# Attention probabilities and values in row tiles of 32 instead of 64, with the banks and one queue's loads rearranged

## The chip, the cores and the metric

The kernel runs on one core of one Trainium2 chip. The metric is the device time of one execution in microseconds; three executions of the kernel before took 294.55, 294.67 and 294.55 us, median 294.55 us. PE is TensorE (its weight loads are PEld), DVE is VectorE, ACT is ScalarE, POOL is GpSimd, SP is the engine whose queue issues every DMA of this kernel.

## The reference

Eight batches of 256 queries attend to 77 context rows each (16 heads of 64, model width 256), then pass a gated feed-forward layer of hidden width 768. Cut to what matters:

```
x = x + tanh(gate) * (softmax((LN(LN(x)) @ w_q) @ (ctx @ w_k).T / 8) @ (ctx @ w_v) @ w_out + b_out)
x = x + (silu(LN(x) @ wg.T) * (LN(x) @ wu.T)) @ wd.T
```

## The kernel before

Everything is float32; where a product is made of three rounded ones (hi times hi, lo times hi, hi times lo), the operands were split into `_hi` and `_lo` by ACT and by DVE or POOL. w_q and w_k are folded with the context into `t_all` ahead of the loop, so the scores of a batch are `xn` times `t`. V is computed once, stored to a scratch tensor in DRAM, and loaded again batch by batch.

A round of the loop treats one batch: its attention, the feed-forward layer of the batch before, and the first scores of the batch after. The order on each engine is written out by hand as a list of stage names (PE_ORDER, DVE_ORDER, ACT_ORDER, POOL_ORDER, SP_ORDER; the names ending in FIRST, START and END hold the order of the first and last rounds). Each engine works through its list strictly in that order, and waits on semaphores counted per batch.

A batch's attention has four units u: head group g = u // 2 (8 heads each) and query half t = u % 2. Per unit:
- S (`scores`, PE, lines 822 to 830): two halves of 4 heads x 77 keys, 6 matmuls each, into one bank of PSUM each. `score_bank` takes SCORE_BANKS in turn; a half waits until DVE has subtracted out of the bank's previous user.
- M (`maxima`, DVE, lines 1375 and 1380): the maxima of both halves, then both subtractions into `probs`. E (ACT, line 1075): the exponential. Z (`sums`, DVE, lines 1389 and 1392): sum and reciprocal.
- P (`normalise`, POOL, lines 1245 and 1253): multiplies by the reciprocals. Two neighbouring heads make a row of 154 keys, whose middle 128 are transposed as they lie (`probs`), and whose 13 at either end go to `rest`.
- T (`transpose_probs`, PE, lines 845 and 848): four transposes and one for the rest, C (ACT, lines 1086 and 1090) copies them to `pt`.

Per head group, V (`values`, PE, line 863) multiplies by the values: 16 float32 products of a 64-row (or 52-row) by 64-column tile of values with 256 queries, each of which the trace shows as two weight loads and two matmuls, 32 per call. They go to banks 4 and 5 (`ps_p`). O0 and O1 of ACT and DVE (lines 1102 and 1400) split the result into `o_hi` and `o_lo`; O0 and O1 of PE (`project`, lines 990 to 994) project it.

G0 to G5 (`gate_up`, line 921, 8 matmuls each), H (`hidden`, DVE, lines 1416 and 1419; the buffer of two makes H wait for POOL's h, line 1271, of two before), D (`down`, lines 974 and 977) and Y (DVE, line 1439) are the feed-forward layer. X1T and XT (lines 888 and 879) transpose the two normalised inputs, LN1 and LN of DVE (lines 1489 and 1432) make them, X1 of DVE (line 1406) splits the first of them. These users share three banks, MISC_BANKS, in the order of PE_ORDER; `last_user` says what each must wait for.

SP's queue, in SP_ORDER: RES loads the residual (line 557), V the values of the next batch (lines 586 and 595, once the present batch's V1 has read the old ones), LN the next input `x_ln` (line 562), OUT stores a result (line 571). In the start, `load_v(0)` is interleaved with the stores of V's five row blocks (line 648); ACT's copy of the last row block (line 1046) reuses the room of the third and waits until its store has landed.

Of the kernel before, what the change touches and what calls it, by code (L numbers as in the profile page):

```python
# [23 lines left out]
F32 = mybir.dt.float32  # L24
# [12 lines left out]
MISC_BANKS = (6, 7, 3)  # L37
SCORE_BANKS = (0, 1, 2)
LAST_BANKS = (4, 5, 7, 6, 0, 1)
LAST_X1T_BANKS = (0, 2)  # L40
LAST_DOWN_BANKS = (2, 3)
# [11 lines left out]
DVE_ORDER = "LN1 M2 LN Z2 X1 M3 O0 H0 Z3 H1 H2 M0 H3 H4 O1 Z0 H5 M1 R0 Z1 R1 AG Y0 Y1".split()  # L53
# [27 lines left out]
V_BANKS = (4, 5, None, 2, 3, 4, 5, 4, 3, None)  # L81
# [8 lines left out]
def xattn_ffn_kernel(nc, x, ctx_in, ln_gamma, ln_beta, w_q, w_kv, w_out, b_out, gate,  # L90
# [31 lines left out]
    NEXT = HALVES * K  # L122
    assert KEYS_WHOLE + NEW == K
    V_LOADS = HALVES + HG
    assert HALVES * KEYS_WHOLE == P and 0 < HR * NEW <= KEYS_WHOLE
# [8 lines left out]
    with whole:  # L134
# [52 lines left out]
        with before_loop:  # L187
# [6 lines left out]
            sb("gap", [P, 160 + 2 * IC * D], where=before_loop)  # L194
# [15 lines left out]
        v_rest = sb("v_rest", [P, 2, HR * DH])  # L210
# [5 lines left out]
        sb("pt_gap", [P, (HG - HR - 1) * Q - ROOMS * P])  # L216
# [16 lines left out]
        hid = sb("hid", [P, 2, Q])  # L233
        stats = sb("stats", [P, NT, 6])
# [61 lines left out]
        shared = [n for n in PE_ORDER if n in ("X1T", "XT", "G0", "G1", "G2", "G3", "G4", "G5", "D0", "D1", "O0", "O1")]  # L296
        bank = {n: MISC_BANKS[i % len(MISC_BANKS)] for i, n in enumerate(shared)}

        def last_user(b, name):

            at = shared.index(name) - len(MISC_BANKS)
            while at >= 0:
                n, k = shared[at], int(shared[at][1]) if shared[at][1].isdigit() else 0
                if n == "XT" and not (isinstance(b, int) and b >= B - 1):
                    return xn_done, DC * (b + 2)
                if n[0] == "O" and not (isinstance(b, int) and b == B):
                    return x1_done, NT * b + k + 1
# [104 lines left out]
        def gate_up_psum(b, f):  # L412

            return ps[:, LAST_BANKS[f], :] if last(b) else ps[:, bank[f"G{f}"], :]

# [123 lines left out]
        def _(sp):  # L539
# [33 lines left out]
            def load_v_whole(n):  # L573
# [9 lines left out]
                whole_keys = (slice(NEW, K), slice(0, KEYS_WHOLE))  # L583
                for r in range(HALVES):
                    half = slice(r * KEYS_WHOLE, (r + 1) * KEYS_WHOLE)
                    sp.dma_start(v_whole[half].rearrange("k g (j d) -> k (g j) d", d=DH),
                                 v_rows[whole_keys[r]].rearrange("k (h r d) -> k r h d", r=HALVES, d=DH)[:, r]).then_inc(v_in, 16)

            def load_v_rest(n, r, heads=range(HR)):
                v_rows = v_scratch.rearrange("(b k) n -> b k n", k=K)[n]  # L590
                by_head = v_rows.rearrange("k (g j r d) -> k r j g d", g=2, r=HALVES, d=DH)
                rest_keys = (slice(0, NEW), slice(KEYS_WHOLE, K))
                for j in heads:
                    first = r * KEYS_WHOLE + j * NEW
                    sp.dma_start(v_rest[first:first + NEW, :, j * DH:(j + 1) * DH], by_head[rest_keys[r], r, j]).then_inc(v_in, 16)

            def load_v(n):
                load_v_whole(n)
                for r in range(HALVES):
                    load_v_rest(n, r)  # L600
# [34 lines left out]
            out_rows = w_out.rearrange("(g n e r d) m -> e g r d n m", g=2, e=2, r=HALVES, d=DH)  # L635

            def load_wo(*which):
                for i in which:
                    for e in range(2):
                        sp.dma_start(wo_raw[e * DH:(e + 1) * DH, 2 * i:2 * i + 2, :],  # L640
                                     out_rows[e, i // HALVES, i % HALVES]).then_inc(s_in["wo"], 16)

            load_ln(1)
            load_wo(0, 1, 2)
            for r in range(RC):
# [4 lines left out]
                if r == 0:  # L650
                    load_wo(3)
                if r == 1:
                    sp.wait_ge(s_vrow[0], 16)
                    load_v_whole(0)
                    load_v_rest(0, 0, range(HR - 1))
                if r == 2:
                    load_v_rest(0, 0, range(HR - 1, HR))
                    load_v_rest(0, 1, range(HR // 2))
                if r == 3:
                    load_v_rest(0, 1, range(HR // 2, HR))  # L660
# [9 lines left out]
        def _(pe):  # L670
# [136 lines left out]
            def scores(b, u):  # L807
# [6 lines left out]
                if isinstance(b, int) and b == 0 and u == 1:  # L814
                    evacuated(pe, first_v + V_BANKS.index(SCORE_BANKS[2]))
# [17 lines left out]
            def transpose_probs(b, g, t):  # L833
# [10 lines left out]
                for j in range(HR):  # L844
                    ins = nc.tensor.transpose(ps_p[:, 0, j * P:(j + 1) * P], probs[:, u, j * NEXT + NEW:j * NEXT + NEW + P], ident[:])  # L845
# [4 lines left out]
            def values(b, g):  # L850
# [5 lines left out]
                for pair in range(2):  # L856
                    for keys in (v_whole, v_rest):
                        for e in range(2):
                            j = 2 * pair + e
                            at = j if keys is v_whole else HR  # L860
                            for r in range(HALVES):
                                half = slice(r * KEYS_WHOLE, r * KEYS_WHOLE + (KEYS_WHOLE if keys is v_whole else HR * NEW))
                                ins = mm(ps_p[e * DH:(e + 1) * DH, r, pair * Q:(pair + 1) * Q],  # L863
                                         keys[half, g, j * DH:(j + 1) * DH], pt[half, at, :],
# [714 lines left out]
```

## Time and profile before

| | |
|---|---|
| median of three executions | 294.55 us |
| the profiled execution | 294.75 us |
| its span, first to last instruction | 292.9 us |
| one steady round | 28.28 us |
| PE busy in the span | 97% |
| DVE, POOL, ACT busy | 79%, 59%, 54% |

What lies between 292.9 and 294.75 us is before the first and after the last instruction. Matmuls overlap each other by design (a matmul's start to the next one's is shorter than its duration), so starts are what to compare on PE. The granted TensorE clock is full in all 40 slices.

### The profile page before, as it was taken

The numbers are of one execution on the slowest core, as the hardware profiler recorded it, in microseconds if no ns is written. First come the engines' busy times: TensorE is split into PE (matmuls) and PEld (weight loads), VectorE is DVE, ScalarE is ACT, GpSimd is POOL, SyncE is SP. The second block draws the span as 40 slices with busy tenths as digits, with TensorE's granted clock in tenths as the row PEclk, the third lists the DMA queues.
The fourth block names the chain that finished last, engine by engine and source line by source line (L and its number), as shares of the span: only waits on it lengthen the run. The fifth ranks groups of instructions, "written<-read, shape, count | busy, mean of one in ns | idle before, by whom it ended". The sixth has DMA issues, their size and how long they took to land.

```text
span 292.9 us, 6761 instructions
## 1 busy us (share of the span) xinstructions
PE 283.7 (97%) x2513; PEld 261.9 (89%) x2513; DVE 230.9 (79%) x609; ACT 157.3 (54%) x311; POOL 173.3 (59%) x199
## 2 busy tenths in 40 slices
PE   8999999999789999999999999999999999999995
PEld 7999978878788899989898989898989899988994
DVE  1598897787778689878986898789778987885873
ACT  3657875567047733863385349435932683156052
POOL 2644875369668690968196639654964587237133
PEclk9999999999999999999999999999999999999999
DMA  6995138522414013001201120112011101110001
GB/s 201 374 369 169 36 106 256 175 71 110 147 43 145 3 42 110 1 23 37 97 0 39 43 74 0 40 41 74 1 41 49 66 3 40 42 36 2 0 32 46
DMA packets 26668, 23.32 MB, mean 80 GB/s; under 512 B 12602, under 2 KB 24866, under 8 KB 26634
## 3 DMA queue, kind: packets, MB, share of 16 engines
q1 hardware_dynamic: 26634, 22.86, 25.1%
q8 instruction: 22, 0.36, 0.5%
q14 instruction: 12, 0.10, 0.1%
HBM read 15.87 MB, written 4.62 MB: 70 GB/s over the span
## 4 chain that ended last, share of the span: by engine, by line
PE 90%; DVE 5%; ACT 1%; issue 1%; POOL 0%; DVEq 0%
PE ps L921 12%; PE ps L863 10%; PE ps L822 6%; PE ps L830 6%; PE ps L826 6%; PE ps L990 5%; PE ps L994 5%; PE ps L991 5%; PE ps L746 5%; PE ps L845 4%; PE ps L974 3%; PE ps L977 3%; PE ps L942 2%; PE ps L754 2%; PE ps L756 2%; PE ps L755 2%
## 5 line engine op out<-in xcount | busy, mean ns | idle before, releaser
L1245 POOL TENSOR_TENSOR probs<-probs,total 128x512 f32<-128x512 f32 x32 | 33.6, 1050 | 60.6 <-DVE total L1392 60.5
L1260 POOL TENSOR_TENSOR t_lo<-t_all,t_hi 128x1232 fp32r<-128x1232 f32 x16 | 45.7, 2857 | 3.0 <-ACT t_hi L1114 3.0
L1271 POOL TENSOR_TENSOR h_lo<-hid,h_hi 128x256 fp32r<-128x256 f32 x42 | 30.7, 738 | 21.1 <-ACT h_hi L1158 21.1
L1086 ACT COPY pt<-ps 128x512 f32<-128x512 f32 x32 | 19.1, 597 | 40.3 <-PE ps L845 40.3
L990 PE MATMUL ps<-wo_hi,o_hi 128*128 128x256 f32 x128 | 36.4, 284 | 0.0
L991 PE MATMUL ps<-wo_lo,o_hi 128*128 128x256 f32 x128 | 36.1, 282 | 0.0
L994 PE MATMUL ps<-wo_hi,o_lo 128*128 128x256 f32 x128 | 35.9, 281 | 0.0
L1102 ACT CAST o_hi<-ps 128x512 fp32r<-128x512 f32 x32 | 17.2, 590 | 25.1 <-PE ps L863 25.1
L822 PE MATMUL ps<-t_hi,xn_hi 128*128 128x308 f32 x128 | 30.7, 321 | 0.0
L1389 DVE TENSOR_REDUCE total<-probs 128x8 f32<-128x616 f32 x32 | 25.3, 791 | 6.3 <-ACT probs L1075 5.5
L1375 DVE TENSOR_REDUCE top<-ps 128x4 f32<-128x308 f32 x64 | 28.3, 471 | 2.3 <-PE ps L830 2.3
L1075 ACT ACTIVATE probs<-probs 128x616 f32<-128x616 f32 x32 | 23.2, 726 | 12.2 <-DVE probs L1380 12.2
L1400 DVE TENSOR_TENSOR o_lo<-ps,o_hi 128x512 fp32r<-128x512 f32 x32 | 20.6, 685 | 10.7 <-ACT o_hi L1102 10.2
L830 PE MATMUL ps<-t_hi,xn_lo 128*128 128x308 f32 x128 | 28.5, 304 | 0.0
L826 PE MATMUL ps<-t_lo,xn_hi 128*128 128x308 f32 x128 | 28.4, 303 | 0.0
L1380 DVE TENSOR_TENSOR probs<-ps,top 128x308 f32<-128x308 f32 x64 | 27.3, 467 | 0.0
L1158 ACT CAST h_hi<-hid 128x256 fp32r<-128x256 f32 x42 | 17.9, 426 | 14.5 <-DVE hid L1419 14.5
L990 PEld LDWEIGHTS ps<-wo_hi,o_hi 128*128 128x128 f32 x128 | 24.0, 187 | 0.4 <-issue 0.4
L994 PEld LDWEIGHTS ps<-wo_hi,o_lo 128*128 128x128 f32 x128 | 24.3, 190 | 0.0
L991 PEld LDWEIGHTS ps<-wo_lo,o_hi 128*128 128x128 f32 x128 | 24.1, 188 | 0.0
L1416 DVE SCALAR_TENSOR_TENSOR hid<-tanh_g,ps 128x256 f32<-128x256 f32 x42 | 17.0, 404 | 8.2 <-POOL h_lo L1271 4.6
L822 PEld LDWEIGHTS ps<-t_hi,xn_hi 128*128 128x128 f32 x128 | 20.2, 189 | 2.9 <-issue 2.7
(171 smaller groups left out, 836.3 us busy)
## 6 DMA issues: line engine op xcount, KB each, us to landing
x_ln<-in_x SPq DMA_DIRECT2D x8, 256.0 KB, 2.9
v_scratch<-v_out SPq DMA_DIRECT2D x4, 512.0 KB, 3.4
v_whole<-v_scratch SPq DMA_DIRECT2D x16, 128.0 KB
stream<-in_x SPq DMA_DIRECT2D x8, 256.0 KB, 3.5
x_rooms<-in_x SPq DMA_DIRECT2D x7, 256.0 KB, 7.8
out<-stream SPq DMA_DIRECT2D x7, 256.0 KB, 2.2
wk_raw<-in_L_xattn_w_kv SPq DMA_DIRECT2D x4, 256.0 KB, 5.2
wq_raw<-in_L_xattn_w_q SPq DMA_DIRECT2D x1, 1024.0 KB, 7.6
```

The lines of the kernel that those rows point to most:

```text
L822: mm(o, xn_hi[:, c, qs], t_hi[:, c, cols], start=c == 0, stop=False)
L826: mm(o, xn_hi[:, c, qs], t_lo[:, c, cols], start=False, stop=False)
L830: ins = mm(o, xn_lo[:, c, qs], t_hi[:, c, cols], start=False, stop=c == DC - 1)
L863: ins = mm(ps_p[e * DH:(e + 1) * DH, r, pair * Q:(pair + 1) * Q], keys[half, g, j * DH:(j + 1) * DH], pt[half, at, :], start=keys is v_who ...
L921: ins = mm(o[:, at:at + Q], whole(w[:, c, fs], general), whole(x2[:, c, :], general), start=x2 is x2_hi and c == 0, stop=x2 is x2_lo and c ...
L990: mm(o, o_hi[:, i, ts], wo_hi[:, i, :], start=i == 0, stop=False)
L991: mm(o, o_hi[:, i, ts], wo_lo[:, i, :], start=False, stop=False)
L994: ins = mm(o, o_lo[:, i, ts], wo_hi[:, i, :], start=False, stop=i == IC - 1)
L1245: nc.gpsimd.tensor_tensor(whole, whole, scale.to_broadcast([P, HR, HALVES, KEYS_WHOLE]), ALU.mult).then_inc(probs_done, 1)
L1260: nc.gpsimd.tensor_tensor(t_lo[:, :, cols], t_all[:, :, n, cols], t_hi[:, :, cols].bitcast(F32), ALU.subtract).then_inc(tlo_done, 1)
L1271: nc.gpsimd.tensor_tensor(h_lo[:, f, :], hid_of(b, f), h_hi[:, f, :].bitcast(F32), ALU.subtract).then_inc(hlo_done, 1)
L1375: nc.vector.reduce_max(top[:, u, heads[r]], psum[r], AXIS_X).then_inc(max_done, 1)
```

## The change

The keys of a batch are no longer split as 64 and 13 in pairs of heads, but as 64 = 2 x 32 (`a`) and 13. The four row quarters `c` of a tile hold four heads: `packed` (two new buffers, by turns) holds 8 heads x 32 keys of half 0 in its first 256 columns and of half 1 in the last 256; a transposed 128-column block is then four heads' 32 keys. `rest` puts two heads' 13 keys into each quarter. V makes 24 products of 32 rows x 64 columns instead of 16 of 64 or 52: each quarter c writes its own bank (the V entry of MISC_BANKS, and 3, 4, 5), its two heads e the upper and lower 64 partitions. The scores have two banks instead of three. V0 and V1 join the users of MISC_BANKS. H3 is moved ahead of M0 on DVE. SP loads `v_whole` in 8 DMAs of 32 rows instead of 2 of 64; `v_rest` stays at 8.

```
-MISC_BANKS = (6, 7, 3)
-SCORE_BANKS = (0, 1, 2)
+MISC_BANKS = (6, 7, 2)
+SCORE_BANKS = (0, 1)
+VALUE_BANKS = (3, 4, 5)
...
-DVE_ORDER = "LN1 M2 LN Z2 X1 M3 O0 H0 Z3 H1 H2 M0 H3 H4 O1 Z0 H5 M1 R0 Z1 R1 AG Y0 Y1".split()
+DVE_ORDER = "LN1 M2 LN Z2 X1 M3 O0 H0 Z3 H1 H2 H3 M0 H4 O1 Z0 H5 M1 R0 Z1 R1 AG Y0 Y1".split()
...
-V_BANKS = (4, 5, None, 2, 3, 4, 5, 4, 3, None)
+V_BANKS = (4, 5, None, 3, 7, 4, 5, 4, 3, None)
...
-        shared = [n for n in PE_ORDER if n in ("X1T", "XT", "G0", ...)]
+        shared = [n for n in PE_ORDER if n in ("X1T", "XT", "V0", "V1", "G0", ...)]
...
+                if n[0] == "V":
+                    return olo_done, NU * b + 2 * k + 1
...
-                for r in range(HALVES):
-                    half = slice(r * KEYS_WHOLE, (r + 1) * KEYS_WHOLE)
-                    sp.dma_start(v_whole[half]..., v_rows[whole_keys[r]]...).then_inc(v_in, 16)
+                for a in range(PARTS):
+                    for c in range(HR):
+                        sp.dma_start(v_whole[quarter(c), a].rearrange("k (f d) -> k f d", d=DH), by_bank[a, c]).then_inc(v_in, 16)
...
-                    ins = nc.tensor.transpose(ps_p[:, 0, j * P:(j + 1) * P], probs[:, u, j * NEXT + NEW:j * NEXT + NEW + P], ident[:])
+                    ins = nc.tensor.transpose(ps_p[:, 0, j * P:(j + 1) * P], packed[(NU * b + u) % ROOMS][:, j * P:(j + 1) * P], ident[:])
...
-                for pair in range(2):
-                    for keys in (v_whole, v_rest):
-                        for e in range(2):
-                            for r in range(HALVES):
-                                ins = mm(ps_p[e * DH:(e + 1) * DH, r, pair * Q:(pair + 1) * Q],
-                                         keys[half, g, j * DH:(j + 1) * DH], pt[half, at, :],
-                                         start=keys is v_whole, stop=keys is v_rest)
+                claim(b, f"V{g}")
+                for a in range(PARTS):
+                    for c in range(HR):
+                        for e in range(HALVES):
+                            mm(ps[e * DH:(e + 1) * DH, value_bank(g, c), 0:Q],
+                               v_whole[quarter(c), a, (HALVES * g + e) * DH:(HALVES * g + e + 1) * DH],
+                               pt[quarter(c), HALVES * a + e, :], start=a == 0, stop=False)
+                for c in range(HR):
+                    for e in range(HALVES):
+                        ins = mm(ps[e * DH:(e + 1) * DH, value_bank(g, c), 0:Q],
+                                 v_rest[quarter(c), g, e * DH:(e + 1) * DH], pt[quarter(c), HR, :], start=False, stop=True)
...
-                    nc.scalar.copy(o_hi[:, 2 * n:2 * n + 2, :],
-                                   ps_p[:, i, :].rearrange("p (i q) -> p i q", i=2)).then_inc(ohi_done, 1)
+                    nc.scalar.copy(o_hi[:, value_chunks(g, i), :], value_psum(g, i)).then_inc(ohi_done, 1)
...
-                nc.gpsimd.tensor_tensor(whole, whole, scale.to_broadcast([P, HR, HALVES, KEYS_WHOLE]),
-                                        ALU.mult).then_inc(probs_done, 1)
+                wait(pool, pt_done, n + 1 - ROOMS)
+                nc.gpsimd.tensor_tensor(packed[n % ROOMS][:].rearrange("p (a h k) -> p h a k", a=PARTS, h=HG), whole,
+                                        scale.to_broadcast([P, HG, PARTS, ROWS]), ALU.mult).then_inc(probs_done, 1)
```

`value_chunks` and `value_psum` give the first copy of each group one bank (256 columns) and the second three (768), where both had 512; DVE's split follows them. `load_wo` brings w_out's rows in the new order of heads with 4 DMAs instead of 8. The rotation of MISC_BANKS becomes X1T 6, V0 7, XT 2, G0 6, G1 7, G2 2, G3 6, G4 7, G5 2, V1 6, O0 7, O1 2, D0 6, D1 7; it was X1T 6, XT 7, G0 3, G1 6, G2 7, G3 3, G4 6, G5 7, O0 3, O1 6, D0 7, D1 3.

## Rows read from the trace of the kernel before

**Rows 1.** The page: busy time of the engines, share of the span, instructions.
```profile
PE 283.7 (97%) x2513; PEld 261.9 (89%) x2513; DVE 230.9 (79%) x609; ACT 157.3 (54%) x311; POOL 173.3 (59%) x199
```
**Rows 2.** Busy time by stretch: one steady round (us, PE, PEld, DVE, ACT, POOL, granted clock, DMA).
```profile
139.60:167.90 28.30, 28.30 (x262) 26.44 (x262) 23.61 (x66) 15.42 (x32) 17.89 (x18) 1.00 0.14 39
```
**Rows 3.** Timeline of PE around one call of V (start us, us, engine, line, ...).
```profile
127.37 0.66 PE L863 MATMUL ps<-pt,v_whole 64*64 64x256 f32 x8
127.86 0.61 PE L863 MATMUL ps<-pt,v_rest 52*64 52x256 f32 x8
128.29 0.61 PE L863 MATMUL ps<-pt,v_whole 64*64 64x256 f32 x8
...
129.27 0.41 PE L822 MATMUL ps<-t_hi,xn_hi 128*128 128x308 f32 x1
```
**Rows 4.** The same call, first 0.05 us and first 0.2 us alone: weight loads, matmuls.
```profile
127.37 0.15 PEld L863 LDWEIGHTS ps<-pt,v_whole 64*64 64x64 f32 x4
127.37 0.45 PE L863 MATMUL ps<-pt,v_whole 64*64 64x256 f32 x4
```
**Rows 5.** Timeline of SP's queue after V1 of a steady round.
```profile
129.40 1.24 SPq L586 DMA_DIRECT2D v_whole<-v_scratch  x2
...
137.36 0.51 SPq L562 DMA_DIRECT2D x_ln<-in_x  x1
```
**Rows 6.** By line: SP's time to issue (min/median/max ns); 13, 64, 128 partitions.
```profile
L595 SPq DMA_DIRECT2D v_rest<-v_scratch x64: 782/782/935, 48.6 to 249.7; - x64
L586 SPq DMA_DIRECT2D v_whole<-v_scratch x16: 538/600/1314, 47.3 to 243.1; - x16
L562 SPq DMA_DIRECT2D x_ln<-in_x x7: 368/512/513, 38.6 to 222.2; - x7
```
**Rows 7.** The page: DMA issues, KB, us from issue to landing.
```profile
x_ln<-in_x SPq DMA_DIRECT2D x8, 256.0 KB, 2.9
```
**Rows 8.** Timeline of DVE in the first third of a steady round.
```profile
142.50 0.85 DVE L1380 TENSOR_TENSOR probs<-ps,top 128x308 f32<-128x308 f32 x2
143.27 0.73 DVE L1432 TENSOR_SCALAR x_hat<-x_ln,mean,rstd 128x256 f32<-128x256 f32 x2
144.14 0.80 DVE L1389 TENSOR_REDUCE total<-probs 128x8 f32<-128x616 f32 x1
145.09 0.64 DVE L1406 TENSOR_TENSOR x_lo<-ps,x_hi 128x512 fp32r<-128x512 f32 x1
146.41 0.85 DVE L1380 TENSOR_TENSOR probs<-ps,top 128x308 f32<-128x308 f32 x2
```
**Rows 9.** Lines by form (count, busy us, mean ns): one subtraction; a split of 256 columns.
```profile
L1380 DVE TENSOR_TENSOR probs<-ps,top 128x308 f32<-128x308 f32 x64 | 27.3, 467 | 0.0
L1524 DVE TENSOR_TENSOR x_lo<-ps,x_hi 128x256 fp32r<-128x256 f32 x2 | 0.8, 422 | 0.0
```
**Rows 10.** Timeline of PE in the same third: S3 and G0 begin.
```profile
142.80 0.53 PE L822 MATMUL ps<-t_hi,xn_hi 128*128 128x308 f32 x2
146.99 0.49 PE L921 MATMUL ps<-x_hi,wg 128*128 128x256 f32 x2
```
**Rows 11.** The chain that ended last: G0 to G2 of one round (start us, us).
```profile
118.95 2.86 PE ps L921 x24
```
**Rows 12.** Timelines of DVE (H3) and PE (V1) of a steady round.
```profile
155.13 0.42 DVE L1416 SCALAR_TENSOR_TENSOR hid<-tanh_g,ps 128x256 f32<-128x256 f32 x1 [0.57 <-POOL h_lo L1271]
155.59 0.42 DVE L1419 TENSOR_TENSOR hid<-hid,ps 128x256 f32<-128x256 f32 x1
...
155.65 0.66 PE L863 MATMUL ps<-pt,v_whole 64*64 64x256 f32 x8
```
**Rows 13.** Timelines of ACT and PE in the start.
```profile
54.41 0.59 ACT L1046 COPY v_out<-ps 104x512 f32<-104x512 f32 x1 [1.36 <-DMA v_scratch<-v_out]
...
56.83 0.59 ACT L1086 COPY pt<-ps 128x512 f32<-128x512 f32 x1
...
57.57 0.63 PE L845 MATMUL ps<-ident,probs 128*128 128x128 f32 x4
```

More of the change, by code:

```diff
@@ L193, in xattn_ffn_kernel @@
             kt_lo = sb("kt_lo", [P, IC, CR], F32R, where=before_loop)
-            sb("gap", [P, 160 + 2 * IC * D], where=before_loop)
+            sb("gap", [P, 2 * IC * D - 96], where=before_loop)
             wg_raw = sb("wg_raw", [P, FC, D], where=before_loop)
@@ L292, in xattn_ffn_kernel @@
         xres_biased, xnlo_done = sem("xres_biased"), sem("xnlo_done")
-        shared = [n for n in PE_ORDER if n in ("X1T", "XT", "G0", "G1", "G2", "G3", "G4", "G5", "D0", "D1", "O0", "O1")]
+        shared = [n for n in PE_ORDER if n in ("X1T", "XT", "V0", "V1", "G0", "G1", "G2", "G3", "G4", "G5", "D0", "D1", "O0", "O1")]
         bank = {n: MISC_BANKS[i % len(MISC_BANKS)] for i, n in enumerate(shared)}
@@ L412, in gate_up_psum, with value_bank, value_psum, quarter @@
         def gate_up_psum(b, f):
-            return ps[:, LAST_BANKS[f], :] if last(b) else ps[:, bank[f"G{f}"], :]
+            if last(b):
+                return ps[:, LAST_BANKS[f], :]
+            return ps[:, FORMER_GATE_BANK if b == B - 1 and f == FC - 1 else bank[f"G{f}"], :]
+        def value_bank(g, j):
+            return bank[f"V{g}"] if j == 0 else VALUE_BANKS[j - 1]
+        def value_psum(g, i):
+            at = bank[f"V{g}"] if i == 0 else VALUE_BANKS[0]
+            return ps[:, at:at + (1 if i == 0 else HR - 1), 0:Q]
+        def quarter(c):
+            return slice(c * ROWS, (c + 1) * ROWS)
+        def value_chunks(g, i):
+            return slice(HR * g, HR * g + 1) if i == 0 else slice(HR * g + 1, HR * (g + 1))
         def tile(t):
@@ L634, in _ @@
             sp.wait_ge(s_job, last_t + 1)
-            out_rows = w_out.rearrange("(g n e r d) m -> e g r d n m", g=2, e=2, r=HALVES, d=DH)
+            out_rows = w_out.rearrange("(g e c d) m -> g e d c m", e=HALVES, c=HR, d=DH)
             def load_wo(*which):
-                for i in which:
-                    for e in range(2):
-                        sp.dma_start(wo_raw[e * DH:(e + 1) * DH, 2 * i:2 * i + 2, :],
-                                     out_rows[e, i // HALVES, i % HALVES]).then_inc(s_in["wo"], 16)
+                for g in which:
+                    for e in range(HALVES):
+                        sp.dma_start(wo_raw[e * DH:(e + 1) * DH, g * HR:(g + 1) * HR, :], out_rows[g, e]).then_inc(s_in["wo"], 16)
             load_ln(1)
-            load_wo(0, 1, 2)
+            load_wo(0)
             for r in range(RC):
@@ L650, in _ @@
                 if r == 0:
-                    load_wo(3)
+                    load_wo(1)
                 if r == 1:
@@ L855, in values @@
                     pe.wait_ge(v_in, 16 * V_LOADS * (b + 1))
-                for pair in range(2):
-                    for keys in (v_whole, v_rest):
[L858 to L862, printed above, removed]
-                                ins = mm(ps_p[e * DH:(e + 1) * DH, r, pair * Q:(pair + 1) * Q],
-                                         keys[half, g, j * DH:(j + 1) * DH], pt[half, at, :],
-                                         start=keys is v_whole, stop=keys is v_rest)
+                if isinstance(b, int) and b == 0 and g == 0:
+                    evacuated(pe, last_v)
+                claim(b, f"V{g}")
[6 more added lines that the diff above has]
+                for c in range(HR):
+                    for e in range(HALVES):
+                        ins = mm(ps[e * DH:(e + 1) * DH, value_bank(g, c), 0:Q],
+                                 v_rest[quarter(c), g, e * DH:(e + 1) * DH], pt[quarter(c), HR, :], start=False, stop=True)
                 ins.then_inc(pv_done, 1)
@@ L928, in gate_up_last @@
                     pe.wait_ge(x2hi_done, B + 1)
-                if LAST_BANKS[f] == bank["G5"]:
+                if LAST_BANKS[f] == FORMER_GATE_BANK:
                     pe.wait_ge(hid_done, FC * (B - 1))
```

82 lines of the change are left out of this document (42 added, 40 removed).

## The prediction

> **What bounds the kernel now.** I read the page first: PE is busy 97% of the span [rows 1]. The table by stretches says whether that is even: in a steady round of 28.28 us PE is busy all 28.30 us of the window at full clock, while DVE has 4.7 us free and POOL 10 us [rows 2]. So PE sets the time, and each change is worth what it does to the distance between PE's starts; everything else counts only when PE comes to wait for it. DVE is the engine to watch: it works in a fixed order and is over 80% full, so lateness at one stage is handed to the next few. SP is not in that table, but its queue is in order too, and three of its users wait behind the loads of V.
>
> **The value products.** One call has 32 matmuls whose starts come in fours: the first four start within 0.02 us (0.45 us together, of which one takes 0.43), and their four weight loads within 0.02 us as well (0.15, one takes 0.13) [rows 4]. A later group of eight starts 0.43 us after the one before, so four start every 0.217 us, and the next stage starts 1.90 us after the call's first matmul [rows 3]: 8 x 0.217 and 0.16 of turning over at both ends. Four is the number of 64 x 64 tiles. The change has 24 products, 48 matmuls, on eight tiles: if all eight run side by side it is 6 x 0.217 = 1.30 us, and 0.16, and 0.03 because eight starts spread wider than four: 1.49 us. That saves 0.41 us per call, 16 x 0.41 = **-6.5 us**. The bounds: nothing is gained by more than that, since a matmul still streams 256 queries; on the other side no row shows quarter tiles, so four at a time (12 groups, 2.76 us) or worse is open. I take eight: there are only two row halves, so four at once should be both column halves too (unless two matmuls of one product share a tile), and the number at once would follow the number of tiles.
>
> **The queue.** V is now 8 issues of 32 partitions where it had 2 of 64. Those two took 1.24 us [rows 5]; by line, 64 partitions take 0.60 (0.54 at least), 13 partitions 0.78, x_ln's 128 take 0.37 to 0.51 [rows 6]. 32 partitions lie between 64 and 13; I take 0.61, near the end of v_whole's own issues, whose pieces and strides are the same. With the 0.04 between issues it is 8 x 0.65 = 5.2 us against 1.3: **3.9 us later** for all that is queued behind (range: 0.40 an issue gives 2.2, 0.78 gives 5.3). The Trainium skill, "DMA: Bandwidth & Descriptors", section on why a DMA increments its semaphore by 16, says that the number of engines is the largest up to 16 that divides the slowest dimension, and that the sequencer itself writes the rest of the increment. By it 32 partitions go like 64 and 13 are the odd ones, so the sum stays at 0.61; no row here shows 32.
>
> Who is behind: x_ln was issued at 137.36 and landed 2.9 us later [rows 5, 7], at 140.3; DVE reads it at 143.27 [rows 8]. 3.0 us of slack against 3.9: DVE now stands still for 0.9 us, of which 0.14 is won back in a gap before the next sum [rows 8], so 0.76 stays. V itself must land too: its last issue then ends at 137.3 + 3.9 = 141.2, with x_ln's 2.9 for the way it is there at 144.1, and V0 starts 12 matmuls after S3's 142.80 [rows 10], at some 144.7. It just fits; at 0.70 an issue it does not, by 0.2.
> In DVE's order X1 and M3 follow, then O0. The new banks make two of them PE's business. G0 sits in X1T's bank and must wait for x_lo before its first matmul: x_lo ends at 145.73 + 0.76 = 146.5, and G0 would start at 146.99 - 0.41 + 0.2 (below) = 146.8 [rows 8, 10]: free still. G1 sits in V0's bank and waits for the first o_lo. M3 ends at 147.26 [rows 8], now 148.0; a split of 256 columns takes 0.42 [rows 9], and with 0.1 for two handoffs G1 can go at 148.5. PE would have it at 146.8 + 8 x 0.119 [rows 11] = 147.7. **0.8 us in each of the 6 rounds** that read such an x_ln: +4.8. Were x_ln in time, this wait would be some 0.15.
>
> **The start.** The 3.9 us also sit between the first and the third store of V's rows. ACT's last copies wait for the landing of that third store with no slack (idle 1.36 us for it), the copy of the transposed probabilities is queued behind them at 56.83, and PE's next transposes start at 57.57 just after it [rows 13]. All move by the same amount: **+3.9**.
>
> **The banks.** S3 has only two banks: its first half waits until M2's first subtraction has emptied one. That starts at 142.50 and takes 0.47 [rows 8, 9], and with 0.06 of handoff S3 starts at 143.03 instead of 142.80 [rows 10]: 0.2 x 7 = **+1.4**. V1 takes G3's bank and waits for H3, which ends at 156.01, because it waited for POOL's h_lo and not for M0; V1 started at 155.65 [rows 12]. With the handoff it is 0.42 us; V0's gain moves both sides alike. Six rounds: **+2.5**. H3 ahead of M0 lets DVE idle some 1.7 us longer there (M0's four operations, twice the 0.85 of a pair [rows 8]) and takes them after, before H4, O1 and H5; O1 on PE waits for H5. Between 0 and 0.5 us; DVE idles 0.57 and more in this stretch [rows 12], so I take 0.2 x 6 = **+1.2**.
> Nothing: POOL's multiply (same elements), the copies (256 and 768 columns for twice 512), the transposes, w_out's loads. DVE and ACT cover them, and each has slack there.
>
> **Sum**, against the profiled execution of 294.75 us (span 292.9 and 1.85 around it): -6.5 + 4.8 + 3.9 + 1.4 + 2.5 + 1.2 = +7.3, 302.1 us. The median of the runs lies 0.2 lower: **301.9 us**. The price of an issue moves it most: at 0.70 G0 waits too, the rounds cost 9.0 and the start 4.6, 307; at 0.78 it is some 311.
>
> **Rivals.**
> A cheap issue (0.40 us): x_ln is in time. The rounds' wait falls to 0.9, the start to 2.2: 294.75 - 6.5 + 0.9 + 2.2 + 5.1 = 296.5. For it: x_ln's own issue takes 0.37 to 0.51. Against: 64 partitions never took below 0.54.
> The tiles do not run side by side, so the change does not do what it says. In the new order both column halves of a quarter come one after the other (c outer, e inner). If a quarter takes one product at a time and matmuls start in order, 12 of the 24 wait for their neighbour: 13 groups of 0.217 and 0.16, 2.98 us, +1.09 a call where I have -0.41. That is +24 us, 326. For it: the order before alternated the row halves. Against: four weight loads of a call start together [rows 4] while only two row halves exist. The Trainium skill, "TensorE: Matmul & The Clock Gate", Part 3 (the mechanism), says that a weight load overlaps running matmuls only where the row group differs and that matmuls start strictly in order. By that rule this rival is the case; the trace speaks against its first half here, and cannot show the second.
> **Faster**: the queue's time goes with descriptors. v_whole's two issues describe 512 pieces each, the eight 128 each. Below 0.2 us an issue nothing is late in the start or in G1; what stays is bank waits, 5.1 us at my sizes, against -6.5. If they come out at half, since each is a difference of under half a microsecond between two engines, it is 294.75 - 6.5 + 0.3 + 2.6 = 291 us. It decides at 0.9 us of waits a round. Against: the 13-partition loads describe 26 pieces and take longest.
> **No change**: the same with the bank waits at full size, 294 to 295.
>
> **Chances.** My forecast with its prices up to 0.78: 0.6. Cheap issue 0.13. Tiles in turn 0.1. Faster 0.12, no change 0.05. Slower by over 0.2% (what a measurement of this kernel can tell from none) is the sum of the first three. The range, 295 to 311, leaves out the faster case and the tiles in turn; its upper end is the price of 0.78.
>
> **What would show it.** Line 863's successor with 48 matmuls a call and 1.49 us to the next stage's start; at 2.8 or more the rival of the tiles holds. SP's eight v_whole issues: 5.2 us together; 3.2 or less and the cheap rival holds. x_ln issued 12 us after V1's end instead of 8. Waits of PE that were not there: V1's matmul for DVE hid (0.4 each), line 921 for o_lo (0.8), scores for the subtraction (0.2), one transpose in the start for ACT's copy (about 4). DVE waiting for the DMA of x_ln, 0.9 a round. If PE shows none of these waits, the bank reasoning was wrong; if the total is under 294, the queue's.

## The result and the profile after

The changed kernel took 305.6 us (median of 4 runs, 304.2 to 308.7) against 294.6 us for the kernel before, a ratio of 1.038 with a 95% interval of 1.032 to 1.045. The profiled execution of after took 305.77 us, its span is 304.1 us where before's was 292.9: the 11.2 us between these two spans are what has to be explained.

The page, busy time of the engines (as [rows 1]), and the table by stretches for three steady rounds (us, then busy time of PE, PEld, DVE, ACT and POOL, granted clock, DMA; as [rows 2]):

```profile
PE 282.4 (93%) x2769; PEld 260.5 (86%) x2769; DVE 230.3 (76%) x609; ACT 157.9 (52%) x311; POOL 172.7 (57%) x199
```
```profile
145.89:175.79 29.90, 28.40 (x294) 26.44 (x293) 23.40 (x66) 15.61 (x32) 17.86 (x18) 1.00 0.14 38
175.79:204.51 28.72, 28.18 (x294) 26.42 (x293) 23.43 (x66) 15.50 (x32) 17.82 (x18) 1.00 0.14 40
204.51:233.48 28.97, 28.18 (x294) 26.41 (x293) 23.43 (x66) 15.50 (x32) 17.81 (x18) 1.00 0.15 40
```

PE fell from 97% to 93% of a longer span. Before, every steady round took 28.28 us and PE was busy in all of it. Now rounds take 28.7 to 29.9 us, PE is busy for 28.2 to 28.5 of them, and no two are alike. So the matmuls don't account for it; PE waits. This is what it waited for, in the whole execution (us in total, times, longest):

```profile
PE ps L886 <- DVE hid L1446: 3.1, 7, 1.2
PE ps L948 <- DVE o_lo L1428: 3.0, 6, 0.6
PE ps L868 <- ACT pt L1113: 2.2, 1, 2.2
PE ps L886 <- DMA v_rest<-v_scratch: 1.5, 1, 1.5
PE ps L948 <- DVE x_lo L1433: 1.5, 2, 0.9
```

L886 is the first matmul of a value call, L948 the gates, L868 the transposed probabilities. The first row is V1 in G3's bank, the second G1 in V0's bank, the third the start, the fourth the first round, and the last G0 in X1T's bank; the kernel before had none of them. The list hardly shows S3's wait in its two banks, since a matmul's end overlaps the start of the next. It shows in the starts, X1T and then S3, before ([rows 10] for S3) and after:

```profile
142.45 0.60 PE L888 MATMUL ps<-ident,x_hat 128*128 128x128 f32 x4
```
```profile
148.68 0.60 PE L915 MATMUL ps<-ident,x_hat 128*128 128x128 f32 x4
149.33 0.55 PE L845 MATMUL ps<-t_hi,xn_hi 128*128 128x308 f32 x2
```

S3 starts 0.65 us after X1T where it was 0.35.

**The value products** came out as hoped for. PE around one call (start us, us), and the first 0.05 us of the same call alone (as [rows 3] and [rows 4]):

```profile
181.15 1.12 PE L886 MATMUL ps<-pt,v_whole 32*64 32x256 f32 x32
182.06 0.64 PE L891 MATMUL ps<-pt,v_rest 32*64 32x256 f32 x16
182.63 0.66 PE L906 MATMUL ps<-ident,x_hat 128*128 128x128 f32 x4
```
```profile
181.15 0.17 PEld L886 LDWEIGHTS ps<-pt,v_whole 32*64 32x64 f32 x8 [0.19 <-issue]
181.15 0.47 PE L886 MATMUL ps<-pt,v_whole 32*64 32x256 f32 x8
```

182.63 - 181.15 = 1.48 us for 48 matmuls, where 32 had taken 1.89 or 1.90. Eight matmuls start within 0.05 us.

**The queue.** SP's queue in a steady round (as [rows 5]), its issue times by line (as [rows 6]; min/median/max ns), and the page's time to landing (as [rows 7]):

```profile
135.37 6.08 SPq L615 DMA_DIRECT2D v_whole<-v_scratch  x8
141.49 6.65 SPq L623 DMA_DIRECT2D v_rest<-v_scratch  x8
148.18 0.51 SPq L591 DMA_DIRECT2D x_ln<-in_x  x1
```
```profile
L615 SPq DMA_DIRECT2D v_whole<-v_scratch x64: 586/599/1594, 46.5 to 257.0; - x64
```
```profile
x_ln<-in_x SPq DMA_DIRECT2D x8, 256.0 KB, 3.1
```

An issue takes 0.60 us, so eight take 5.1, as in most rounds. In this round one of them took 1.59 and the eight 6.1. DVE and PE in the same round (as [rows 8] and [rows 10]):

```profile
148.80 0.86 DVE L1408 TENSOR_TENSOR probs<-ps,top 128x308 f32<-128x308 f32 x2
151.51 0.74 DVE L1459 TENSOR_SCALAR x_hat<-x_ln,mean,rstd 128x256 f32<-128x256 f32 x2 [1.85 <-issue]
153.11 0.64 DVE L1433 TENSOR_TENSOR x_lo<-ps,x_hi 128x512 fp32r<-128x512 f32 x1
...
155.21 1.28 DVE L1428 TENSOR_TENSOR o_lo<-ps,o_hi 128x256 fp32r<-128x256 f32 x2
```
```profile
153.89 0.48 PE L948 MATMUL ps<-x_hi,wg 128*128 128x256 f32 x2 [0.53 <-DVE x_lo L1433]
155.68 0.50 PE L948 MATMUL ps<-x_hi,wg 128*128 128x256 f32 x2 [0.60 <-DVE o_lo L1428]
```

Here x_ln is issued at 148.18 and is there 3.1 us later, at 151.3. DVE stands still for 1.85 us before it can use it. What is behind it in DVE's order is late by nearly as much (x_lo follows it in 1.60 us where it took 1.82), so G0 waits for x_lo and G1 for the first o_lo.

**The first round** is the worst one. SP's queue there before, then SP's queue and DVE after:

```profile
73.49 1.94 SPq L586 DMA_DIRECT2D v_whole<-v_scratch  x2
...
82.18 0.51 SPq L562 DMA_DIRECT2D x_ln<-in_x  x1
```
```profile
75.86 5.71 SPq L615 DMA_DIRECT2D v_whole<-v_scratch  x8
81.60 7.41 SPq L623 DMA_DIRECT2D v_rest<-v_scratch  x8
89.06 0.51 SPq L591 DMA_DIRECT2D x_ln<-in_x  x1
```
```profile
92.08 0.73 DVE L1459 TENSOR_SCALAR x_hat<-x_ln,mean,rstd 128x256 f32<-128x256 f32 x2 [4.78 <-DMA x_ln<-in_x]
```

x_ln's load went out at 82.18 before and at 89.06 now; DVE waits 4.8 us for it, and PE waits 1.5 for v_rest, 0.9 each for x_hat and x_lo, 0.6 for o_lo and 0.5 at S3.

**Where the 11.2 us came from**, by the times at which PE starts its stages: up to the first project of the first round (75.53 before, 75.54 after) nothing; from there to the first steady round (111.38, 116.39) 5.0; in the five rounds up to the last T0 (252.78, 262.86) 5.1; from there to the end 1.1.

### The profile page after: what moved, and what is told of

Its sections match the earlier page's. It is cut to its first block, busy times and chain, and to the rows that moved or that the text cites. A ratio compares the mean times of both kernels' runs of the same rounds, so it can differ in the third digit from the quotient of the medians.

```text
span 304.1 us, 7357 instructions
## 1 busy us (share of the span) xinstructions
PE 282.4 (93%) x2769; PEld 260.5 (86%) x2769; DVE 230.3 (76%) x609; ACT 157.9 (52%) x311; POOL 172.7 (57%) x199
## 4 chain that ended last, share of the span: by engine, by line
SPq 26%; PE 23%; POOL 21%; DVE 10%; DMA 9%; issue 6%; ACT 3%; DVEq 0%; ACTq 0%; POOLq 0%
SPq L623 14%; SPq L615 12%; DMA x_ln<-in_x 6%; POOL t_lo L1288 6%; PE ps L771 5%; POOL h_lo L1299 3%; POOL stream L1313 3%; PE ps L886 3%; POOL packed_odd L1276 2%; POOL xn_lo L1293 2%; DVE total L1417 2%; DMA v_scratch<-v_out 2%; POOL packed_even L1276 2%; PE ps L969 2%; DMA ctx_raw<-in_ctx 2%
## 5 line engine op out<-in xcount | busy, mean ns | idle before, releaser
L1276 POOL TENSOR_TENSOR packed_even<-probs,total 128x512 f32<-128x512 f32 x16 | 16.9, 1053 | 59.8 <-DVE total L1420 59.8
L1403 DVE TENSOR_REDUCE top<-ps 128x4 f32<-128x308 f32 x64 | 27.6, 471 | 2.3 <-PE ps L853 2.3
L1129 ACT CAST o_hi<-ps 128x256 fp32r<-128x256 f32 (+1 forms) x32 | 17.2, 588 | 19.3 <-PE ps L891 19.3
L1428 DVE TENSOR_TENSOR o_lo<-ps,o_hi 128x256 fp32r<-128x256 f32 (+1 forms) x32 | 21.4, 688 | 7.0 <-ACT o_hi L1129 6.9
L1184 ACT CAST h_hi<-hid 128x256 fp32r<-128x256 f32 x42 | 17.1, 408 | 13.6 <-DVE hid L1446 13.6
```

What stands on the lines that cost most here:

```text
L1276: nc.gpsimd.tensor_tensor(packed[n % ROOMS][:].rearrange("p (a h k) -> p h a k", a=PARTS, h=HG), whole, scale.to_broadcast([P, HG, PARTS, ...
```

## The experiments

All were timed beside the kernel before, whose medians were 294.9 to 295.2. Times of steady rounds are between starts of T0 on PE.

**The load of x_ln ahead of V's loads.**

```diff
-SP_ORDER = "RES V LN WD OUT".split()
+SP_ORDER = "RES LN V WD OUT".split()
```

> The changed kernel, with x_ln's load ahead of V's loads in SP's order; nothing else. Theory (the queue makes x_ln late, and that makes DVE late for the first o_lo, for which G1 and at times G0 wait): x_ln is issued some 12 us earlier, DVE waits 0 for its DMA, G0 waits 0 and G1 0.15 to 0.3 where they had 0.24 and 0.74 together with x_ln late; a steady round falls from 29.3 to 28.5 us. In the first round the 4.8 us of DVE for x_ln go, the wait of V0 for v_rest grows from 1.5 to 2.1. Total some 299 to 300 us. Rival (the bank shared by V0 and G1 costs this by itself, since X1 and M3 stand ahead of O0 on DVE): G1 keeps 0.6 or more, total 303 or more.

300.1 us, 1.014 of before (1.011 to 1.018). x_ln is now issued long before V. In a steady round PE waits 0.56 us for V1's bank; S3's 0.31 and O1's 0.09 stay. The round (us, PE, PEld, ...) and the load in SP's queue:

```profile
172.28:200.75 28.47, 27.91 (x295) 26.36 (x294) 23.62 (x66) 15.34 (x32) 17.89 (x18) 1.00 0.14 40
```
```profile
176.74 0.37 SPq L591 DMA_DIRECT2D x_ln<-in_x  x1
```
The theory holds: G0 to G2 take 2.94 us again, as before, G0 follows XT in 0.41, and four of the five rounds are equal at 28.47 (the first is 28.63). G1's wait in V0's bank is nothing when DVE is on time. V1's wait grew from 0.37 to 0.56: part of what DVE had been late at G1 was hidden there. In the first round V0's wait for v_rest fell to 1.36, where 2.1 was expected.

**Eight issues in the kernel before.** v_whole by 32 partitions and group; keys and heads go where they went.

```diff
-                    half = slice(r * KEYS_WHOLE, (r + 1) * KEYS_WHOLE)
-                    sp.dma_start(v_whole[half]..., v_rows[whole_keys[r]]...[:, r]).then_inc(v_in, 16)
+                    for q in range(2):
+                        at = r * KEYS_WHOLE + q * KEYS_WHOLE // 2
+                        key = whole_keys[r].start + q * KEYS_WHOLE // 2
+                        for g in range(2):
+                            sp.dma_start(v_whole[at:at + KEYS_WHOLE // 2, g]..., v_rows[key:key + KEYS_WHOLE // 2]...[:, g, r]).then_inc(v_in, 16)
```

> The kernel before, with v_whole brought by eight issues of 32 partitions instead of two of 64; same tiles, banks and matmuls. Theory (the queue costs PE only through the bank that V0 shares with G1, which this kernel does not have): eight issues take 5.1 us, DVE waits some 0.9 us per round for x_ln, but PE waits for nothing new in a steady round, which stays at 28.3 us. Only the start and the first round cost, where V and x_ln are latest: +2 to +4 us, total 297 to 298. Rival (a late x_ln costs PE by itself, through x_hat, M3 or o_lo): +0.5 us or more in each steady round as well, total 300 or more.

298.0 us, 1.009 (1.006 to 1.012), and rounds of 28.28, as the theory had it. Whether for its reason can't be said:

```profile
132.92 3.65 SPq L589 DMA_DIRECT2D v_whole<-v_scratch  x8
136.61 6.60 SPq L598 DMA_DIRECT2D v_rest<-v_scratch  x8
143.26 0.51 SPq L562 DMA_DIRECT2D x_ln<-in_x  x1
```
```profile
L589 SPq DMA_DIRECT2D v_whole<-v_scratch x64: 303/432/907, 47.8 to 249.3; - x64
```

Each issue took 0.43 us and not 0.60, so in the steady rounds x_ln (143.26 and some 3 us of way) was there before DVE asked for it at 146.79. Only the first round has the late load, issued at 87.59:

```profile
91.08 0.73 DVE L1435 TENSOR_SCALAR x_hat<-x_ln,mean,rstd 128x256 f32<-128x256 f32 x2 [1.01 <-DMA x_ln<-in_x]
```

There G0 and G1 wait for nothing, as the theory has it for the old banks. But the sums and M3 stand behind x_ln on DVE too, and from T2 to T3 PE falls 0.8 us behind, so a late x_ln may not be free in the old banks either; one round can't separate it. Of the whole loss, the start has most: the first project starts at 78.23 instead of 75.53 (2.7 later), T0 of the first steady round at 114.90 instead of 111.38 (0.8 more), and from there on nothing changes. So the loss lies in the start and the first round of a kernel that has neither the new tiles nor the new banks.

**DVE's M0 ahead of H3**, as before the change.

```diff
-DVE_ORDER = "... H1 H2 H3 M0 H4 ...".split()
+DVE_ORDER = "... H1 H2 M0 H3 H4 ...".split()
```

> The changed kernel with M0 ahead of H3 on DVE again, as before. Theory (H3 waits for POOL's h_lo in either order, and V1 waits for H3): V1's wait stays at 0.3 to 0.5 us, O1's small wait falls, total within 1 us of the changed kernel's 305.6. Rival (the moved M0 is what keeps H3 early enough for V1's bank): V1 waits 0.7 us or more longer in six rounds, total 309 or more.

306.5 us, 1.039 (1.035 to 1.043): no difference that can be told from after's. V1's wait is as long in most rounds (0.73 in the first steady one), S3's is 0.21 instead of 0.30 and O1's 0.1 us is gone. The place of M0 is worth 0.2 us a round at most and gives it back elsewhere.

**The loops of the value products turned**, column half outside.

```diff
-                    for c in range(HR):
-                        for e in range(HALVES):
+                    for e in range(HALVES):
+                        for c in range(HR):
```

> The changed kernel, with the loops of the value products turned: column half outside, quarter inside, so that four different row quarters follow each other. Theory (eight tiles run side by side in either order): 48 matmuls and 1.48 us to the next stage, total 305.6. Rival (the order decides which tiles overlap): 1.3 us or less, or 1.7 or more, that is 3 us faster or 4 us slower in all.

307.1 us, 1.041 (1.037 to 1.044), within the spread of after's own runs (mean clocks 0.987 to 0.994 in all six, 0.994 to 1.0 in after's four). Every call of a steady round takes 1.48 or 1.49 us again:

```profile
181.17 1.12 PE L886 MATMUL ps<-pt,v_whole 32*64 32x256 f32 x32
...
182.65 0.66 PE L906 MATMUL ps<-ident,x_hat 128*128 128x128 f32 x4
```

182.65 - 181.17 = 1.48: the order in which the eight tiles are served doesn't matter.

**POOL's h1 ahead of the bias.** In e1_ln_first H3's first half starts at 187.73, and POOL is at this (start us, us):

```profile
185.32 0.38 POOL L1282 TENSOR_TENSOR rest<-probs,total 128x104 f32<-128x104 f32 x1
185.65 1.28 POOL L1313 TENSOR_TENSOR stream<-stream,bias 128x512 f32<-128x512 f32 x1
186.88 1.44 POOL L1299 TENSOR_TENSOR h_lo<-hid,h_hi 128x256 fp32r<-128x256 f32 x2
```

```diff
-POOL_ORDER = "P2 Ta X h0 P3 B WO h1 h2 ...".split()
+POOL_ORDER = "P2 Ta X h0 P3 h1 B WO h2 ...".split()
```

> The changed kernel with x_ln's load first (as in e1_ln_first), and on POOL the split h1 ahead of the addition of the bias (B, 1.28 us). In e1_ln_first V1 waits 0.56 us per round for H3, whose first half starts at 187.73 in one round, just after POOL's h_lo of H1 ended at 187.6 behind B. Theory (that h_lo holds H3): H3 starts some 1.2 us earlier, V1 waits for nothing, a round falls from 28.47 to 27.9 us, total 300.1 - 6 x 0.56 = 296.8 us. Rival (H3 waits for ACT's tanh, which the profile names): V1 keeps 0.4 or more, total 299.5 to 300.5.

295.7 us, 1.001 (0.999 to 1.003), better than foretold. V1's wait is gone (2.08 us from G4 to V1, as before), and so is O1's, while S3's fell to 0.21: each of them had been DVE handing its lateness on. The trace puts H3 down to ACT's tanh, but what held it was POOL. The round:

```profile
167.77:195.50 27.73, 27.73 (x294) 26.17 (x293) 23.66 (x65) 15.31 (x32) 17.91 (x18) 1.00 0.15 42
```

PE is busy all through, and the round is 0.55 us shorter than before's: 2 x 0.41 from the value products, less 0.21 for S3 and some 0.06 of small differences.

**The third store of V's rows early.**

```diff
-                    load_v_rest(0, 0, 1, 2)
                 if r == 2:
-                    load_v_rest(0, 3, 4, 5)
+                    load_v_rest(0, 0, 1, 2, 3, 4, 5)
```

> The changed kernel with x_ln's load first, and in the start the third store of V's rows ahead of the first three loads of v_rest instead of behind them. The store is issued 2.5 us earlier, ACT's last V copies and the transposes of T1 too (60.4 to some 58). PE then waits at the first use of the transposed weights in any case, so at 75 us nothing is left of it on PE. Theory (the start reaches the first round only through SP, whose loads of the next V wait for V1): those loads start some 2 us earlier, V0 of the first round too, total 298.1 us. Rival (the gain is used up by the wait for the weights): 300.1 us, no change.

298.15 us, 1.013 (1.010 to 1.017). The foretold 298.1 is met, but hardly by the theory. T1 starts at 58.0, yet at the first project PE is at 74.8, and there it also is without this edit in e5_h1_before_bias, whose T1 starts at 59.5. The 1.5 us are spent on the way: V0 waits 0.7 for v_rest, the transposes of the weights behind it 0.9 where they wait 0.4 in e5, and the next T 0.65 instead of 0.31.

So the rival is nearer in kind. What the median gained over e1_ln_first is mostly that kernel's lower clock, of which more at the end: its two runs at full clock took 297.9 and 298.8 us, the four runs here at 0.997 or more 297.5 to 298.2. At equal clock the edit is worth some 0.5 us, which two runs against four only hint at.

**M2's subtraction between its two reductions.**

```diff
-                for r in range(2):
-                    ...reduce_max(top[:, u, heads[r]], psum[r], AXIS_X)...
+                if u != NT:
+                    for r in range(2):
+                        largest_of(r)
                 ...
                 for r in range(2):
+                    if u == NT:
+                        largest_of(r)
                     dve.wait_ge(max_done, half + r + 1)
```

> The changed kernel with x_ln's load first, and DVE's M2 in the order largest, subtract, largest, subtract (before: both largest, then both subtractions), so that S3's first score bank is free one reduction (0.4 us) earlier. Theory (S3's 0.30 us wait is for M2's first subtraction): it goes, 7 x 0.30 = 2.1 us, a round 28.2, total 298.0 us. Rival (V1's wait for H3 takes it up, since POOL and ACT set H3): V1's wait grows from 0.56 to 0.86, a round stays at 28.47, total 300.1.

300.05 us, 1.017 (1.015 to 1.019): the theory falls, the rival's total comes true, and by another wait than it named. S3 follows X1T in 0.40 instead of 0.66, V1's wait fell to 0.4, and G1 has a new one:

```profile
178.81 0.40 PE L948 MATMUL ps<-x_lo,wu 128*128 128x256 f32 x2
179.34 0.50 PE L948 MATMUL ps<-x_hi,wg 128*128 128x256 f32 x2
```

The next gate starts 0.53 us after this pair, where two pairs within a gate lie 0.24 apart. A PE that is 0.26 us earlier at S3 is so at V0 and G1 too, while DVE's o_lo comes when it did: M3 stands ahead of it on DVE. With O0 ahead of M3, in e11_o0_before_m3, G1 waits for nothing.

**All three.**

> The changed kernel with x_ln's load first and all three edits: h1 ahead of the bias on POOL, the third store early, M2's subtraction between. If each of the three waits is one of its own, the gains add: 300.1 - 3.4 - 2.0 - 2.1 = 292.6 us, a round at 27.6, faster than before (294.6). If they take each other's place, 295 to 298 and PE shows the waits elsewhere (G1 for o_lo, or V0 for v_rest).

293.3 us, 0.995 (0.994 to 0.997): faster than before. Rounds are 27.80, so the split of M2 costs 0.08 here where it should have saved 0.2; G1 waits again.

**Without M2's edit.**

> The changed kernel with x_ln's load first, h1 ahead of the bias on POOL and the third store early; M2 in its own order again. In e8_all_three the round was 27.80 us with M2 split up, in e5_h1_before_bias 27.72 without. Theory (the split of M2 only moves 0.2 us from S3 to G1 and adds 0.1): rounds of 27.72, total 292.8 us, and the spread of the runs narrow, since PE has no wait of over 2 us in the start after which the granted clock can fall. Rival (M2's order saves in the start and end what it costs in the rounds): 293.3 or more.

293.5 us, 0.995 (0.994 to 0.997). Rounds are 27.72, as foretold; the total is the rival's, and 0.3 between e8 and e9 is less than their runs spread. By the first steady T0 M2's edit has gained 0.2 us (111.48 against 111.69), in five rounds it loses 0.4, so at the last T0 e9 is 0.2 ahead (250.30 against 250.48). The profiled executions differ the other way only behind PE's last matmul, so neither order can be called the faster.

**wu's write behind v_whole in the first round.**

```diff
                     weights_in_place(0)
-                    weights_in_place(1)
             ...
                 load_v_whole(n)
+                if isinstance(n, int) and n == 1:
+                    weights_in_place(1)
```

> As e9, and in the first round the write of wu in place goes behind the eight v_whole loads instead of ahead of them (it waits for POOL's wo_lo, at some 74.3 us, with V's loads queued behind it). Theory (V0 of the first round waits 1.4 us for v_rest because SP's queue starts V's loads 2 us after V1 ended): the wait falls to 0, total 291.3 us. Rival (the first weights' write ahead of it, or G's need of wu, sets it): V0's wait stays over 1 us, or a new wait of G0 for wu of 1 to 2 us, total 292.5 to 294.

**292.0 us, 0.989 of before (0.987 to 0.990)**, the fastest of all. V's loads start at 72.45 instead of 74.78 in e9 (75.86 in the changed kernel), straight behind V1:

```profile
72.45 5.22 SPq L614 DMA_DIRECT2D v_whole<-v_scratch  x8
77.86 0.53 SPq L577 DMA_DIRECT2D wu<-wu_t  x1
78.44 7.55 SPq L622 DMA_DIRECT2D v_rest<-v_scratch  x8
```

V0 of the first round follows S3 in 1.90 us, without a wait, where it waited 1.38 in e9. The forecast of 291.3 took e9's forecast as its base; against e9 as measured the edit gave the 1.5 us.

**O0 ahead of M3 on DVE**, with M2 split up.

```diff
-DVE_ORDER = "... X1 M3 O0 H0 ...".split()
+DVE_ORDER = "... X1 O0 M3 H0 ...".split()
```

> The changed kernel with x_ln's load first, h1 ahead of the bias, third store early, M2 split up, and DVE's O0 ahead of M3. Theory (G1 waits 0.3 us for the first o_lo behind M3): it goes, and S3 has no wait either, rounds of 27.5, total 291.7 us. Rival (DVE then stands idle for V0 and ACT's o_hi, with M3 behind it, and T3 or S0 come late by it): rounds of 28 or more, 294 or more.

299.7 us, 1.017 (1.014 to 1.020), rounds of 28.29: the rival, but at another place. S3 and G1 wait for nothing; DVE stands still for ACT's o_hi instead, M3 and H0 come behind, and G3 waits for H0:

```profile
176.56 0.42 DVE L1432 TENSOR_TENSOR o_lo<-ps,o_hi 128x256 fp32r<-128x256 f32 x1 [0.85 <-ACT o_hi L1128]
```
```profile
180.60 0.50 PE L947 MATMUL ps<-x_hi,wg 128*128 128x256 f32 x2 [0.56 <-DVE hid L1450]
```

**The four edits of order on the kernel before.**

> The kernel before with the four edits of order of e10_up_weights_later (x_ln's load first, h1 ahead of the bias, third store early, wu's write behind v_whole) and with its own tiles, banks and value products. Theory (the before kernel has no waits in its rounds for these edits to remove, so all that e10 gains on it comes from the value products, 1.89 to 1.48 us a call): rounds of 28.28 us, total 294.0 to 295.2, against e10's 292.0. Rival (the edits of order gain in the start or the first round of any kernel, and the new tiles add nothing): 292.0 to 293.0.

295.1 us, 1.001 (0.999 to 1.003), rounds of 28.28. The edits do nothing for the old kernel, so the 3.2 us that e10 gains over it come with the change itself: 1.4 up to the first steady T0, 2.8 in the five rounds (2 x 0.41 a round from the value products, less 0.21 for S3 and 0.05 of small differences), and 1.0 lost at the end. The round:

```profile
168.10:196.38 28.28, 28.28 (x262) 26.42 (x261) 23.59 (x65) 15.31 (x32) 17.89 (x18) 1.00 0.14 40
```

## Why the prediction was right, and where it was not

The forecast was 301.9 us in a range of 295 to 311, at 0.83 for slower; 305.6 was measured. The direction and the waits of the steady rounds were right in kind. That the total came so near is luck in two places: up to the first project I was 3.1 us too high and in the first round 4.2 too low, and the price of an issue is right for a wrong reason (below). Term by term, on PE's stage starts in the profile of after (five steady rounds lie between its T0 starts):

| term | forecast | measured |
|---|---|---|
| value products | -0.41 x 16 | 1.48 us for 1.89: -0.41 x 16 |
| an issue of v_whole | 0.61 | 0.60, and 1.0 to 1.6 for some |
| x_ln late at G1 (and G0) | 0.8 a round | G1 0.74, G0 0.24 |
| S3 in two banks | 0.2 | 0.30 |
| V1 in G3's bank | 0.42, six rounds | 0.37, and 1.0 in the last |
| O1 behind M0 | 0.2 | 0.12 |
| a steady round | 29.1 (28.28 + 0.8) | 29.3 |
| the start, at T1 | +3.9 | +2.7 |
| the start, at the first project, two value calls included | +3.1 | 0.0 |
| the first round | +0.8 | +5.0 |
| from the last T0 to the end | -0.6 | +1.1 |

**The queue, the banks and their coupling through DVE** were right. e1_ln_first takes x_ln's lateness away, and a steady round loses 0.8 us with it; e5_h1_before_bias takes H3's away. S3's 0.30 was priced at 0.2 because I took DVE's times of before; DVE was late by 0.09 itself, and e5 measures 0.21 where it isn't. The 0.74 and 0.24 are means that hold something I had not reckoned with, issues that take 1 us and more (see the last section). In the two rounds without one G1 waits 0.45 and 0.71 and G0 nothing, against my 0.8.

**The price of 0.61** was taken from the old v_whole issues, "whose pieces and strides are the same". The pieces are (256 bytes), the strides in DRAM are not: 512 bytes before, 1 KB after. With 32 partitions and the old stride e2_before_eight_issues pays 0.43, close to the rival's 0.40. So the size was right and the ground for it was not.

**"All move by the same amount: +3.9"** is the first step that failed. Third store (51.31 to 54.35), ACT's copies and T1 did move together:

```profile
60.27 0.63 PE L868 MATMUL ps<-ident,packed_odd 128*128 128x128 f32 x4 [2.22 <-ACT pt L1113]
```

But by 2.7 us (0.6 of which PE was late before any changed part), since w_out's loads, costed at nothing, are four issues where they were eight: 3.85 us of the queue instead of 6.2, and V's loads started at 46.50 instead of 47.30. And I stopped following PE there. By the first project two value calls had taken 0.8 off, which my sum had too. A wait that the kernel before had at 75.14 had gone as well:

```profile
PE ps L767 <- DVE wd_t L1318: 1.7, 1, 1.7
```

In the first round the places of the gates and downs on PE are used for transposing the weights, in the same banks. D0's shared its bank with G5's, one place ahead, and waited for DVE to empty it. With V0 and V1 in the rotation it shares it with G3's and V1's. G3's was emptied long before, and DVE's split of V1's bank (73.96 to 74.38) is done before PE comes at 75.18. 2.7 - 0.8 - 1.8 is about the 0 at 75.5. e2_before_eight_issues, which is as late in T1 (60.3) and keeps the old banks, still has this wait (1.69) and starts the first project at 78.23, 2.7 after before's. I had read the rotation for the waits that it adds and not for those that it takes away.

**"The rounds" taken as alike** is the second, and the dearer one. The first round is not a steady one. There V's loads stand behind the write of wu, which waits for POOL's wo_lo, and x_ln's load behind both went out at 82.18. The change moved the start of these loads by 2.4 us (from 73.49 to 75.86) and put 4.5 on top, 6.9 in all. That costs 5.0 us where I had a steady round's 0.8. e1_ln_first takes 2.9 of it away (from the first project to the first steady T0 it needs 37.9 us, the changed kernel 40.9, the kernel before 35.9), e10_up_weights_later the last 1.5. In the old kernel e2_before_eight_issues, whose load goes out at 87.59, loses only 0.8 in this stretch. The rest belongs to what that run doesn't have: the dearer issues, the new banks and the new tiles. The rows for the queue were in the trace of before.

**V1 in "six rounds"** is the third: the last block has no S0 and S1, so only a few matmuls lie between G3 and V1, and the wait for the hidden half is longest there:

```profile
277.54 0.83 PE L886 MATMUL ps<-pt,v_whole 32*64 32x256 f32 x17 [1.16 <-DVE hid L1446]
```

The end of the kernel is 1.1 us longer, where my terms make it shorter.

**The rivals.** Cheap issues (0.40 us) are out, at 0.60. The tiles in turn are out, at 1.48 us; e6_half_outer shows it for both orders. The rule of the Trainium skill that I set beside this rival ("TensorE: Matmul & The Clock Gate", Part 3), that a weight load overlaps only where the row group differs, doesn't hold here in that form: in the call shown the second eight weight loads run from 181.20 to 181.38, while the first eight matmuls, which use all four row groups, run until 181.57 and later. The same page, section "Why this matters for your kernels", has it better: tiles that differ in row and column run together, with a span of one matmul and 4 ns for each further one. The estimate by its figure is 0.43 + 7 x 0.004 = 0.46 us here, and the trace agrees at 0.47. The faster rival (291 us) is out for the kernel as changed, though e10_up_weights_later, which keeps every part of the change and moves four steps, is at 292.0.

## What to carry to other kernels

An in-order DMA queue is a resource with a due time for each user: before splitting a load into more issues, write down who stands behind it and by when each is needed, in the first and last round as well as a steady one. Sharing a bank with a stage whose reader is an in-order engine couples PE to all that stands ahead of that reader; the waits it makes are then best removed at their source (a load, a split on POOL moved by one place), not at the bank. And a wait that is removed only pays if the next engine in line is early too: of the edits of order here those to a DMA queue and to POOL paid, and those to DVE gave their gain back within a few stages.

## What was not expected of the hardware

**The price of an issue** isn't set by partitions and pieces alone. e2_before_eight_issues and the changed kernel both issue v_whole as 32 partitions of four pieces of 256 bytes; the one takes 0.43 us, the other 0.60. They differ in the spacing of the pieces in DRAM (512 bytes and 1 KB). Whether the spacing sets it wasn't tried.

**Stretched issues.** A few issues take 0.9 to 1.9 us instead of 0.60 or 0.78, and always at nearly the same places of SP's queue. In all eleven traces with the new tiles the 95th or 96th issue (v_whole) is one and so is one of the 152nd to 155th (v_whole); in most the 84th or 85th and the 141st or 142nd (v_rest) are too. After the change these are at 137.29 (1.59 us), 226.34 (1.00) and 113.78 (1.22), in e1_ln_first at 135.22 (1.40), 221.43 (1.35) and 112.56 (1.27). In the steady rounds of before and of e2_before_eight_issues no issue of V takes over 0.85. What stretches an issue stays open.

They order the steady rounds of after. x_ln's load goes out 1.94, 2.29, 1.48, 1.57 and 1.88 us after T0, and the rounds take 29.50, 29.90, 28.72, 28.97 and 29.38: the three long ones have an issue of 1 us or more in the loads ahead of x_ln, the two short ones don't. In e1_ln_first, where x_ln goes ahead of V, four of the five rounds are equal all the same. So it is the missing slack that lets a stretched issue through to PE.

**The clock after a wait.** In e1_ln_first PE waits 2.45 us for T1 in the start. After it the granted clock is at 0.52, the lower of its two levels (1.2 of 2.4 GHz), for 3.5 us:

```profile
60.39 0.66 PE L868 MATMUL ps<-ident,packed_odd 128*128 128x128 f32 x4 [2.45 <-ACT pt L1113]
```
```profile
60.86:64.39 3.53, 3.53 (x17) 3.53 (x16) 1.76 (x4) 1.48 (x3) 0.68 (x1) 0.52 0.92 227
```

From T1 to V0 it takes 4.4 us there and 2.8 in the profile of after, whose clock stayed up after a wait of 2.22 us: 1.6 us more. The length of the wait alone doesn't decide it: in the profile of e2_before_eight_issues PE waits 2.66 us there, and the granted clock stays at 1.00. Mean clocks of 0.991 to 0.994 are found in two of after's four runs and in seven of twelve of e5_h1_before_bias (295.2 to 296.8 us; its four fastest, at 293.8 to 294.0, have 0.997 or more, though a fifth run with 0.997 took 295.75). None of e9's and e10's runs, whose T1 doesn't wait, is below 0.997, and e10's spread over 0.6 us; but two of e6b's six are at 0.994 (300.2 and 300.5 us), and its T1 doesn't wait in its profile either. The profile of e6_half_outer has another occasion: after the first round's waits (1.8 us for v_rest, 0.7 for x_hat, 0.9 for x_lo, 0.6 for o_lo) the granted clock is 0.50 from 96.5 to 99.9. So a part of what the waits cost is no wait of PE but the clock behind them.
